# Moving one subtraction and four bit unpackings inside the drain between the two layers of a graph kernel

## The reference, cut to what matters

```python
# layer 0: neighbours of the same class only
w   = adj * (y @ y.T)
z0  = x + 0.9 * (w @ x) / max(sum(abs(w), 1), 1e-12) + 0.1 * h0
x1  = layernorm(z0)
# layer 1: all neighbours. adj is 0 or 1, no row has more than 350 of them,
# so the kept values are tanh(1) times adj
f   = tanh(x1 @ W_proj + b_proj) @ W_gcn
out = layernorm(x1 + relu(tanh(1) * (adj @ f) + b_gcn))
```

## The kernel before, in words

| step | TensorE, in order | VectorE, in order |
|---|---|---|
| 42 | transpose 37, x4, W_gcn 36, W_proj 37, x6 | low half 35, four unpackings for 41, normalise 38, six operations of block 39, four unpackings for 41 |
| 43 | transpose 38, x4, W_gcn 37, W_proj 38, x8 | low half 36, normalise 39, eight unpackings for 42 |
| 44 | transpose 39, x3, W_gcn 38, W_proj 39, x10 (product 41) | low half 37 |
| 45 | W_gcn 39, x10 (product 41) | low half 38 |
| 46 | waits for all 40 low halves, then ends products 40 and 41 | low half 39 |

## Time and profile before

### The profile page before, as it was taken

How to read it: one execution, slowest core, us unless ns; L and a number is a source line. 1 busy time by engine, 2 the same in 40 slices (tenths; PEclk the granted TensorE clock), 3 DMA queues, 4 the chain that set the end, 5 groups by cost and what they waited for, 6 DMA issues and landing times.

```text
span 457.6 us, 15126 instructions
## 1 busy us (share of the span) xinstructions
PE 432.3 (94%) x5116; PEld 384.4 (84%) x5116; DVE 375.1 (82%) x1363; ACT 265.3 (58%) x358; POOL 160.0 (35%) x310
## 2 busy tenths in 40 slices
PE   3679999999999999999999998999999999999995
PEld 2457898898888888888988897888888888888884
DVE  6988899999999999999999986775656656656654
ACT  4997799998999999999999953960000000000000
POOL 4021353455544455544455543122122122122121
PEclk9997999999999999999999999999999999999999
DMA  8999999999999999999999800000000000000000
GB/s 265 340 405 417 421 394 372 425 417 419 417 416 419 421 424 422 420 425 421 422 421 422 338 3 1 8 17 19 13 17 11 17 17 11 17 17 11 17 18 20
DMA packets 25744, 108.68 MB, mean 238 GB/s; under 512 B 5281, under 2 KB 15682, under 8 KB 15714
## 3 DMA queue, kind: packets, MB, share of 16 engines
q1 hardware_dynamic: 25714, 108.30, 59.1%
HBM read 105.73 MB, written 2.56 MB: 237 GB/s over the span
## 4 chain that ended last, share of the span: by engine, by line
PE 81%; DVE 5%; DMA 5%; SPq 4%; issue 3%; ACT 1%; POOL 1%; POOLq 0%; DVEq 0%; ACTq 0%
PE acc L620 68%; PE words L566 7%; DMA a_rows<-in_adj_dram 5%; DVE a_bits L944 2%; PE feat_acc L694 2%; PE proj_acc L703 1%; SPq L413 1%; PE xnt_acc L684 1%; PE xnt_acc L549 1%; DVE turned L1035 1%; ACT count_out L797 1%; SPq L407 1%; DVE z_high L1115 0%; SPq L383 0%; SPq L414 0%
## 5 line engine op out<-in xcount | busy, mean ns | idle before, releaser
L620 PE MATMUL acc<-x_parts,turned 128*128 128x257 f16 x1560 | 188.5, 277 | 3.8 <-DVE turned L1035 3.3
L797 ACT ACTIVATE count_out<-a_rows,ones 128x2688 bf16<-128x2688 f32 (+1 forms) x80 | 190.2, 2377 | 1.0 <-DMA a_rows<-in_adj_dram 0.5
L620 PEld LDWEIGHTS acc<-x_parts,turned 128*128 128x128 fp8e4 x1560 | 152.1, 99 | 26.0 <-issue 4.9
L620 PE MATMUL acc<-f_parts,turned 128*128 128x256 f16 x1520 | 165.6, 271 | 0.0
L620 PEld LDWEIGHTS acc<-f_parts,turned 128*128 128x128 fp8e4 x1520 | 146.9, 98 | 16.9 <-issue 0.2
L944 DVE TENSOR_SCALAR a_bits<-a_rows 128x2688 bf16<-128x2688 f32 x78 | 113.7, 1458 | 3.7 <-DMA a_rows<-in_adj_dram 3.4
L1035 DVE TENSOR_SCALAR turned<-a_words 128x320 uint16 (+1 forms) x305 | 66.3, 231 | 56.5 <-PE acc L620 52.9
L485 POOL TENSOR_TENSOR var_eps<-mean_var,consts 128x1 f32<-128x1 f32 x79 | 18.4, 233 | 256.3 <-DVE mean_var L1298 130.9
L488 POOL TENSOR_TENSOR rstd<-var_eps,consts 128x1 f32<-128x1 f32 x79 | 84.3, 1067 | 6.2
L902 ACT ACTIVATE xn_t<-acc,bg_col,consts 128x8 f32<-128x8 f32 x1 | 0.4, 357 | 147.3 <-PE acc L733 147.3
L1035 DVE TENSOR_SCALAR turned<-same_class 128x320 uint16<-128x320 uint16 x312 | 70.8, 252 | 0.1
(11 more groups left out here) (143 smaller groups left out, 315.5 us busy)
## 6 DMA issues: line engine op xcount, KB each, us to landing
a_rows<-in_adj_dram SPq DMA_DIRECT2D x39, 1344.0 KB, 7.6
a_rows<-in_adj_dram SPq DMA_DIRECT2D x39, 1156.0 KB, 8.1
out_dram<-xn SPq DMA_DIRECT2D x39, 64.0 KB, 1.5
h_rows<-in_L_gnn_h_dram SPq DMA_DIRECT2D x19, 128.0 KB, 8.0
xs<-in_x_dram SPq DMA_DIRECT2D x3, 640.0 KB, 9.3
xs<-in_x_dram SPq DMA_DIRECT2D x1, 512.0 KB, 10.8
y_nat<-in_L_gnn_y_dram SPq DMA_DIRECT2D x1, 304.0 KB, 3.6
f_parts<-in_adj_dram SPq DMA_DIRECT2D x3, 40.0 KB
```

The costliest lines, as they stand in the source:

```text
L620: mm = pe.matmul((acc1 if second else acc)[par][0:m, low:cols], bits, parts[:, b, low:cols], start=first and b == blocks[0], stop=last and ...
L797: act.activation(count_out[0:m, 0:w], a_rows[par][h][0:m, 0:w], ACT.Relu, bias=ones[0:m, 0:1], scale=-HUGE, accum_out=col).then_inc(s_coun ...
```

## The change

Two things are moved on VectorE, and none is added or removed. The low half of block 36 is computed at step 42, right after the normalisation of block 38, instead of at the start of step 43. The last four unpackings for product 41 stood after `row_moments` of block 39 (step 42); now one stands behind each of `row_scale`, `row_inverse`, `add_high` and `add_low` of block 39.

```diff
-                if valid(t - 7):
+                if valid(t - 7) and not (isinstance(t, int) and t == NB + 3):
                     low_features(t - 7, rows_of(t - 7))
...
                 if valid(t - 4):
                     normalize_block(t - 4, par)
+                if isinstance(t, int) and t == NB + 2:
+                    low_features(t - 6, rows_of(t - 6))
...
                     row_scale(t - 3, odd, m)
                 bits(2, 4)
+                begin(NB + 2, 1, 8, 10)
                 if post:
                     row_inverse(t - 3, m)
                 bits(4, 6)
+                begin(NB + 2, 1, 10, 12)
                 if post:
                     add_high(t - 3, odd, m)
                 bits(6, 8)
+                begin(NB + 2, 1, 12, 14)
                 if post:
                     add_low(t - 3, odd, m)
+                begin(NB + 2, 1, 14, BITS)
...
                 begin(NB, 0, 0, BITS)
-                begin(NB + 2, 1, BITS // 2, BITS)
                 begin(NB + 3, 2, 0, BITS)
```

## The result

The changed kernel is slower: 461.49 us (median of 20 runs, 459.17 to 463.37) against 459.02 us (20 runs, 457.94 to 460.75) for the kernel before. The ratio is 1.0044, 95% interval 1.003 to 1.0057, so 2.0 us, where the prediction had 0.5. The means differ by 2.0 us too, the two medians by 2.5. The forecast range of 458.4 to 460.9 us misses it. Two single runs in what follows, of 856 us in e1 and 2404 us in e3, were disturbed and are left out of every comparison.

A forecast was written before the change was run, and what follows sets the result against it. The drain's chain through the low half of block 37 was taken to bound product 42's start. +0.35 for the low half and +0.15 for four unpackings gave 459.04 + 0.50 = 459.5 us, range 458.4 to 460.9.

The forecast's parts named there:

- The chain: Drain: block 39's six operations, rstd, normalise 39, eight unpackings, low half 37, W_gcn 38 set product 42's start; +0.50 us.
- The wait before W_gcn 37: TensorE's 1.41 us stall in the drain, until low half 36 is written; claimed hidden behind the longer chain.
- What was taken away behind `mean_var` 39: VectorE's four unpackings and low half 36, covered by the wait for rstd; removing them gains 0.
- the low half: Low half 36 ahead of `row_scale` 39 on VectorE, waiting for ScalarE's high half: +0.35 us.
- The four unpackings: One in each gap between block 39's dependent operations on VectorE, mostly hidden: +0.15 us.
- the lower bound: Smallest delay of the drain's chain, with all unpackings hidden and a faster `var_eps`: +0.15 us.
- GpSimd beside an idle VectorE: `var_eps` of block 39 falls to its minimum without VectorE's port interference: 0.06 us less, not taken into the +0.50.
- rival 3: Two TensorE idle times in the drain, about 2.1 us together, make its clock fall: 3.8 us slower, 462.8 us; chance 0.05.

The follow-up runs named there:

- e1: The changed kernel as it is, once more, beside the kernel before: ratio 1.0025.
- e3: Only the four unpackings moved, the low half of block 36 left at the start of step 43, against the kernel before: ratio 1.0003.
- e7: Low halves of blocks 36 and 37 both moved ahead, the four unpackings left in place, against the kernel before: ratio 0.9991.
- e2: Only the low half of block 36 moved, the four unpackings left in place, against the kernel before: 462.23 us, ratio 1.0065.
- e13: The kernel before with 18 matmuls of unused result in TensorE's idle time near the start, as base on another chip: median 458.67 us.
- e5: The kernel before with 18 matmuls of unused result added in TensorE's idle time near the start: 458.43 us, ratio 0.9984.
- e11: Only the low half of block 36 moved, run again, against the kernel before: ratio 1.0025.
- e12: The changed kernel with 18 matmuls of unused result in TensorE's idle time near the start, run again: 459.48 us.
- e14: The changed kernel with 18 unused matmuls in the idle time near the start, beside the kernel before with the same: median 459.40 us.
- e6: The changed kernel with 18 matmuls of unused result in TensorE's idle time near the start: 458.92 us.

## Why the prediction was wrong, point by point

**The chain was right,** in its path and nearly in its size. The wait before W_gcn 37 was in the shadow of the chain through low half 37, and removing it alone gained nothing; e7 shows it from the other side, since moving low half 37 too gained 0.69 us. What was taken away behind `mean_var` 39 was worth 0, as 1.01 us of idle VectorE shows. Of the terms, the low half was put at +0.35 and e2 has +0.33. The four unpackings were put at +0.15: from `row_scale` to `mean_var` of block 39 it took 281.48 - 279.81 = 1.67 us instead of 1.53, so +0.14, of which e3 shows only 0.03 at the end of the chain. One term was named and put into the lower bound alone, and should have been taken: GpSimd beside an idle VectorE. Its instructions after `mean_var` 39 took 0.18 and 0.54 us, where `var_eps` had 0.25 in the trace of before and rstd 0.58.

```profile
281.73 0.18 POOL L485 TENSOR_TENSOR var_eps<-mean_var,consts 8x1 f32<-8x1 f32 x1 [2.41 <-DVE mean_var L1133]
281.99 0.54 POOL L488 TENSOR_TENSOR rstd<-var_eps,consts 8x1 f32<-8x1 f32 x1
```

`var_eps` fell to the minimum of the earlier trace rows, as the Trainium skill's page "SBUF — State Buffer", section "Who interferes with whom", would have it by its rule of one pair of ports that GpSimd shares with some VectorE instructions; the trace agrees with 0.18 us, without showing that the port is the reason. The sum came out at 0.36 to 0.49 us in the four profiles of the changed kernel whose clock held, counted against the 10.89 of before. Against e13's execution of before, with 11.26, it is 0 to 0.12. In all six profiles of the changed kernel `var_eps` took 0.18 us, so the change seems to take away a delay that the kernel before has in some executions. In how many, these profiles are too few to tell.

One bound in the prediction doesn't follow from its own words. With 0.8 us of scatter to either side, 459.2 to 460.0 becomes 458.4 to 460.8, not 458.6 to 460.8. The stated range began at 458.4 anyway.

**The step that failed is the weighing of rival 3,** the fall of TensorE's clock, which the sum put at nothing. The prediction gave it 0.05, because "the longer by itself is shorter than the 1.41 us that did nothing". The longest idle time is not what decides. Behind one of 1.41 us no trace has a fall (before, e5, e13), and none of the 24 runs of before with its start filled took over 459.3 us. Behind two of 1.05 and 0.85 us with 0.65 us of work between them the clock did fall, in four of eight profiles of drains with that pair (e2, e11, e12, e14). Of the runs of the changed kernel with its start filled, 13 of 36 have a mean clock of 0.993 or less; that is a rough count of the same, as one of the 24 runs of before has it too.

Nor do these traces show that the sum decides. The start has counterexamples both ways: in the trace of before TensorE is idle 2.05 us up to 19.39 us, and in that after 2.54 us up to 19.36 us, at a granted clock of 1.00 before and behind; in e12 the clock fell at about 29 us, and the longest idle time in the 9 us ahead of that is 1.03 us. The prediction had the two idle times, their sum and the place right. From one long idle time with a fall and one of 1.41 us without, it could not tell what two short ones would do, and 0.05 was too sure. That some executions would fall and others not was not among its outcomes.

**The price of rival 3 was too high.** It was put at 3.3 us, from the long slow stretch at the start. In e2 the matmul time lost is 0.11 x 2 + 0.50 x 2 + 0.24 x 2 = 1.7 us, and 1.4 of it reach product 42. The stretch is shorter than that at the start; what covers the other 0.3 us was not looked into. So rival 3 was no separate outcome at 462.8 us but a mixture: 1.2 to 1.5 us in a share of the runs (from W_gcn 38 to product 42 it is 7.26 to 7.49 us in the four profiles with a fall, against 6.03).

**How the 2.0 us divide.** With the start filled the change costs 0.5 us (e6 against e5) and 1.1 us (e14 against e13) in the mean. The runs of e14 whose clock held lie 0.3 us over e13 in the median, and the profiles give the chain 0.4 to 0.5 over the shorter chain of before; the falls are the rest. With the start as it is, the means differ by 2.0, 1.0 and 1.9 us in three sets. A mean clock of 0.982 or less, which none of 124 runs of before had, marks 14 of 43 runs of the changed kernel; but a fall in the drain with no or a short one at the start hides among the runs at 0.985 to 0.99, so the true share is higher. One more sign of that: 5 of 43 had 0.992 or more, against 56 of the 124 of before. If three quarters of all runs fell, it would be 0.45 + 0.75 x 1.4 = 1.5 us, most of the 1.7 us by which the 43 runs lie higher in the mean. That share is worked out and not shown: three profiled executions of the changed kernel with its start as it is happened to have no fall in the drain. A part of the difference can also be the end behind the last normalisation, which was longest in two of these three. What decides in which execution the clock falls, and why it seems to happen more often when the start isn't filled, stays open.

## What to carry to other kernels

Before pricing the removal of a stall, go on to the next semaphore and look at the delay from its signal to the instruction: 0.15 us with no wait printed was the sign that a second chain was just as late. When a stall only changes its place, price the new pattern of idle times on TensorE as well, and don't call it safe because its longest idle time is shorter than one that did nothing. A few matmuls whose results nobody reads are a cheap test, and here a cheap cure. Profile a kernel more than once: here the same instructions gave a chain of 10.9 or 11.3 us, an end of 2.4 or 3.9 us, and a clock that fell or held. Where runs scatter by 3 us, look at the mean clock of each run first, remove the common cause in both kernels, and only then compare.

## What the runs showed of the hardware that was not expected

The granted clock fell to its lower level after idle times of 1.02 and 0.85 us with 0.65 us of work between them, with 0.89, 0.50 and 0.76 granted in the stretches of 2 us from 284 us on (e2), in some executions of the same program and not in others (0.50 and 0.67 in e14, 1.00 in e6). An addition of 8x1 on GpSimd beside 16-bit shift-and-mask instructions on VectorE took 0.25 us in two executions of the kernel before and 0.55 us in a third (e13), and 0.18 us in six of the changed kernel, beside an idle VectorE. Eighteen matmuls in one idle time of 2.7 us narrowed the runs of the kernel before from 457.8 to 461.4 us down to 457.7 to 458.9 (e5).
